# Self attention: key, query and output projections as products of 64 stationary columns in two column halves, bias product over 128 rows

## The reference

```python
attn_in = _adaln(x, cond, ln1_w, ln1_b, g1_w, g1_b, b1_w, b1_b)
q = _heads(xq @ wq)
k, v = jnp.split(ctx @ wkv, 2, axis=-1)
...
q = _rope(q, sq, cq)
k = _rope(k, sk, ck)
sim = jnp.einsum('bhnd,bhmd->bhnm', q, k) * DH ** (-0.5)
a = jax.nn.softmax(sim, axis=-1)
o = jnp.einsum('bhnm,bhmd->bhnd', a, v)
o = o.transpose(0, 2, 1, 3).reshape(xq.shape[0], xq.shape[1], MID)
return o @ wo + bo
```

## Time and profile before

| | us |
|---|---|
| median of 3 runs | 2261.14 (2261.02 to 2263.14) |
| profiled execution, its span | 2262.3 |
| PE busy | 2086.6 (92%) |
| VectorE busy | 1797.4 (79%) |
| ScalarE busy | 1379.8 (61%) |
| self attention | 0 to about 1571 |

### The profile page before, as it was taken

How to read it: one execution, slowest core, us unless ns; L and a number is a source line. 1 busy time by engine, 2 the same in 40 slices (tenths; PEclk the granted TensorE clock), 3 DMA queues, 4 the chain that set the end, 5 groups by cost and what they waited for, 6 DMA issues and landing times. The chain is left out here.

```text
span 2262.3 us, 37701 instructions
## 1 busy us (share of the span) xinstructions
PE 2086.6 (92%) x14808; PEld 891.2 (39%) x14808; DVE 1797.4 (79%) x2799; ACT 1379.8 (61%) x1748; POOL 35.0 (2%) x26
## 2 busy tenths in 40 slices
PE   4799999999999999999999999997379999986999
PEld 2233333334333334433333533334233344444676
DVE  5888999986899997799999699974858888844664
ACT  4577777765777765677677477662647665633442
POOL 1000000000000000000000000000400000000000
PEclk8899999999999999999999999999579999987999
DMA  5010101111110200110110111002423333324111
GB/s 187 29 38 30 45 32 57 39 38 38 57 39 29 67 29 29 48 57 32 46 39 30 48 48 48 29 17 68 121 80 106 116 121 120 124 71 135 38 38 38
DMA packets 102102, 135.83 MB, mean 60 GB/s; under 512 B 36693, under 2 KB 75175, under 8 KB 101927
## 3 DMA queue, kind: packets, MB, share of 16 engines
q1 hardware_dynamic: 101927, 133.43, 18.1%
HBM read 67.89 MB, written 13.11 MB: 36 GB/s over the span
## 5 line engine op out<-in xcount | busy, mean ns | idle before, releaser
L929 ACT ACTIVATE sa_probs<-sa_ps_s 128x1024 f32<-128x1024 f32 x512 | 496.3, 1021 | 217.2 <-PE sa_ps_s L721 217.2
L736 PE MATMUL sa_ps_o<-sa_probs,sa_v_pair 128*64 128x512 f32 x2048 | 534.9, 614 | 7.2 <-DVE sa_mx L1070 7.2
L1083 DVE TENSOR_TENSOR sa_acc<-sa_acc,sa_probs 128x1024 f32<-128x1024 f32 x384 | 452.8, 1220 | 18.2 <-ACT sa_probs L929 8.3
L1070 DVE CUSTOM_DVE_ANT_0 sa_rise<-sa_ps_t,sa_rise 128x512 f32<-128x512 f32 x504 | 327.2, 686 | 141.0 <-PE sa_ps_t L698 138.0
L917 ACT ACTIVATE sa_rise<-sa_ps_t 128x1024 f32<-128x1024 f32 x252 | 257.5, 1022 | 166.3 <-PE sa_ps_t L691 166.1
L714 PE MATMUL sa_ps_s<-sa_hi 64*128 64x512 f16 x1024 | 197.0, 378 | 1.5 <-ACT sa_raw L903 1.5
L714 PE MATMUL sa_ps_s<-sa_hi,sa_lo 64*128 64x512 f16 x1024 | 197.1, 378 | 0.0
L714 PE MATMUL sa_ps_s<-sa_lo,sa_hi 64*128 64x512 f16 x1024 | 197.0, 377 | 0.0
L736 PEld LDWEIGHTS sa_ps_o<-sa_probs,sa_v_pair 128*64 128x64 f32 x2048 | 106.6, 135 | 187.9 <-issue 101.0
L691 PE MATMUL sa_ps_t<-sa_kd,sa_hi 64*128 64x512 f16 x504 | 99.6, 389 | 23.0 <-ACT sa_hi L913 7.7
L691 PEld LDWEIGHTS sa_ps_t<-sa_kd,sa_hi 64*128 64x128 f16 x504 | 26.1, 93 | 206.2 <-issue 162.3
(11 more groups left out here) (327 smaller groups left out, 3935.4 us busy)
## 6 DMA issues: line engine op xcount, KB each, us to landing
sa_swp<-sa_raw SPq DMA_DIRECT2D x124, 256.0 KB, 2.4
sa_inv<-sa_scratch SPq DMA_DIRECT2D x128, 128.0 KB, 2.9
ca_swp<-ca_raw SPq DMA_DIRECT2D x64, 256.0 KB, 2.4
ca_inv<-ca_scratch SPq DMA_DIRECT2D x64, 256.0 KB, 3.9
sa_xs<-in_x SPq DMA_DIRECT2D x4, 1024.0 KB, 6.6
sa_xr<-in_x SPq DMA_DIRECT2D x4, 1024.0 KB, 6.5
cap_xs<-x_after_self SPq DMA_DIRECT2D x4, 1024.0 KB, 7.3
x_after_cross<-ca_xr SPq DMA_DIRECT2D x32, 128.0 KB, 2.1
```

What stands on the lines that cost most here:

```text
L736: ins = pe.matmul(ps_o[rows(x), half(c)], v_pair[:, kt, rows(x)], probs[:, kt % 2, c, half(x)], start=(kt == 0), stop=(kt == NK - 1))
L929: act.activation(probs[:, kt % 2, c, :], ps_s[c][:, :], ACT.Exp, scale=float(DH) ** -0.5).then_inc(s_p, 1)
L1070: dve.tensor_tensor_reduce(out=larger, in0=max_banks(j, t)[:, half(x)], in1=larger, scale=1.0, scalar=-3.0e38, op0=ALU.add, op1=ALU.max, a ...
L1083: dve.tensor_tensor(acc[:, c, :], before, probs[:, kt % 2, c, :], ALU.add).then_inc(s_acc[c], 1)
```

## The change

`project` and `output` call a new function that makes each product as two: the stationary operand is cut into columns 0 to 63 and 64 to 127, which write partitions 0 to 63 and 64 to 127 of the same bank. Both stream the same moving operand. The bias product is cut in the same way, and is over 128 rows instead of 2: `bo_rows` and `two_ones` get 128 rows, zero but for the first two, which are set on VectorE at the start (one memset more, two waits changed). `project_v` is not changed. Cross attention and the feed-forward layer are not changed.

```diff
+def split_product_by_halves(pe, out, k_tiles, lhs, rhs, lhs_at, rhs_at, start=True, stop=True):
+    terms = [(k, a, b) for k in k_tiles for a, b in ((0, 0), (1, 0), (0, 1))]
+    for i, (k, a, b) in enumerate(terms):
+        for h in range(2):
+            part = slice(h * DH, h * DH + DH)
+            ins = pe.matmul(out[part], lhs[a][lhs_at(k)][:, part], rhs[b][rhs_at(k)], start=(start and i == 0),
+                            stop=(stop and i == len(terms) - 1))
+    return ins
...
-        bo_rows = sb("bo_rows", [2, D], F16)
+        bo_rows = sb("bo_rows", [P, D], F16)
...
-        two_ones = sb("two_ones", [2, P], F16)
+        two_ones = sb("two_ones", [P, P], F16)
...
-                split_product(pe, projected(j, i, c), range(KD), (wk, wq)[i], xT, lambda k: (slice(None), k, cols),
-                              lambda k: (slice(None), b, k, half(c))).then_inc(s_kq[i], 1)
+                split_product_by_halves(pe, projected(j, i, c), range(KD), (wk, wq)[i], xT,
+                                        lambda k: (slice(None), k, cols),
+                                        lambda k: (slice(None), b, k, half(c))).then_inc(s_kq[i], 1)
...
-                    pe.matmul(y_bank(b, t), two_ones[:], bo_rows[:], start=True, stop=False)
-                return split_product(pe, y_bank(b, t), ks, (o_hi, o_lo), wo, lambda k: (slice(None), k, ts),
-                                     lambda k: (slice(None), k, slice(None)), False, stop)
+                    for x in range(2):
+                        pe.matmul(y_bank(b, t)[rows(x)], two_ones[:, rows(x)], bo_rows[:], start=True, stop=False)
+                return split_product_by_halves(pe, y_bank(b, t), ks, (o_hi, o_lo), wo, lambda k: (slice(None), k, ts),
+                                               lambda k: (slice(None), k, slice(None)), False, stop)
...
-            pe.wait_ge(s_init, 5)
+            pe.wait_ge(s_init, 7)
...
-            act.activation(bo_rows[:], bo_two[:], ACT.Copy, scale=WS).then_inc(s_bhi, 1)
+            act.wait_ge(s_init, 5)
+            act.activation(bo_rows[0:2], bo_two[:], ACT.Copy, scale=WS).then_inc(s_bhi, 1)
...
-            dve.memset(two_ones[:], 1.0).then_inc(s_init, 1)
+            dve.memset(two_ones[:], 0.0).then_inc(s_init, 1)
+            dve.memset(bo_rows[:], 0.0).then_inc(s_init, 1)
...
-            dve.wait_ge(s_init, 4)
+            dve.wait_ge(s_init, 5)
+            dve.memset(two_ones[0:2], 1.0).then_inc(s_init, 1)
```

More of the change, by code:

```diff
@@ L1194, in _ @@
             dve.wait_ge(s_bhi, 1)
-            dve.scalar_tensor_tensor(out=bo_low[:], in0=bo_two[:], scalar=WS, in1=bo_rows[:], op0=ALU.mult,
+            dve.scalar_tensor_tensor(out=bo_low[:], in0=bo_two[:], scalar=WS, in1=bo_rows[0:2], op0=ALU.mult,
                                      op1=ALU.subtract).then_inc(s_blo, 1)
```

## The result

| | before | after |
|---|---|---|
| median of the runs, us | 2262.09 (2261.02 to 2263.14) | 2245.38 (2244.09 to 2246.13) |
| span of the profiled execution, us | 2262.3 | 2242.2 |

The ratio is 0.9924, with a 95% interval of 0.9910 to 0.9938: 16.7 us faster. The prediction was 17.7 us, 2243.4 us for the median. (The kernel before was timed anew with every comparison; its medians lie between 2261.8 and 2263.1 us.)

A forecast was written before the change was run, and what follows sets the result against it. TensorE was taken to set the pace nearly everywhere, VectorE close behind. Ordinary groups 8.6, output groups 7.5 and tiles behind the loop 1.6 us sum to 17.7 us saved: 2243.4 us median, range 2233 to 2253 us.

The forecast's parts named there:

- step 0: Key projection in each group: only the entry's change of form goes, since `totals` (128*32) follows; 0.11 us.
- step 4: Query projection between two calls of `values`: the whole price of the change of form is saved, 0.26 us.
- The bound from below: A pair of column halves takes the full product's own time: 0.217 us at 512 columns, 0.109 at 256.
- Rival A: Weight loads in column halves are not hidden, 0.05 us more a pair: 44 us slower, 2305 us; chance 0.09.
- Steps 1 and 5: Key and query projections in ordinary groups: 0 us each, since ScalarE's chain from `shift` holds the following `differences`.
- Output groups: Groups 9, 17 and 25, which have output tiles: 2.5 us saved in each, 7.5 us in all three.
- Step 2: In groups with output tiles, entered from `project_v`, which stays 128*128, so one stop stays: about 0.20 us saved.
- Steps 3 and 6: In groups with output tiles, two tiles each with their bias products: 0.41 us saved in each step.
- Ordinary groups, the count: Key and query projections outside groups with output tiles: 24 x 0.11 + 23 x 0.26 = 8.6 us.
- Behind the loop: Output tiles after the groups: 2.40 instead of 2.60 us from bias to bias, 0.20 x 8 = 1.6 us.
- rival C: VectorE takes back step 4's gain beyond its gap, at worst 6.0 us: 2249.5 us; chance 0.12.
- Rival B: Float32 and float16 column halves still stop between them; only bias and tile gain, 5 to 6 us: 2255.5 us; chance 0.08.

The follow-up runs named there:

- the moves of `high`: ScalarE's `high` of steps 1 and 5 put before the step's exponentials: 2225.43 us in the changed kernel, 2250.63 us in the kernel before.
- the last run: Changed kernel with `high` before the exponentials, step 2's value projection in column halves, and VectorE's multiplication by the sines behind the next step's maxima: 2228.60 us.
- the run of half after half: Changed kernel, but each projection and output tile makes all products of the first column half, then all of the second: one run, 2333.35 us.

## Why the prediction was right, point by point

- *The stop.* 0.10 us at each change of form and 0.05 us for the first float32 load: the earlier trace rows gave it, and with the form kept, both are gone. An ordinary group is 0.37 us shorter, as forecast, 0.11 in step 0 and 0.26 in step 4.
- *No cost of halves.* The bound from below was right in all three lengths, 0.216, 0.109 and 0.056 us a pair. Rival A, the loads that are not hidden, would have needed 0.016 us a pair and got none. Its 0.05 us for a load, taken from float32 rows, was also too much: where a load of 64 float16 columns is exposed it costs 0.02 us (last section).
- *Steps 1 and 5.* Nothing came of them, for the reason given; the moves of `high` show both that ScalarE's chain held them and that the saving was there behind it.
- *Output groups.* Forecast 2.5 us each, measured 2.35, 2.35 and 2.47. Two terms were mis-sized. Step 2 gave 0.11 us instead of 0.20. There VectorE's residual stands behind two multiplications; with one of them moved away, and the value projection in halves (the last run), the step is another 0.35 us shorter, while the halves alone left it at 8.45 us. In step 0 of groups 9 and 17 nothing came (6.88 and 6.90 us) where 0.11 was counted. Steps 3 and 6 gave 0.43 each instead of 0.41.
- *Ordinary groups, the count.* 8.2 us instead of 8.6. Without group 0, which was counted at 0.37 and can't be told from the unsteady start, 8.2 had been forecast too, and that is luck: two misses of 0.8 us stand against each other. Groups 8, 16 and 24 were counted at 0. The first two gave 0.24 us each, and group 24, which prepares nothing, is an ordinary group and gave 0.36. In groups 3, 4, 11, 12, 19 and 20, around the preparation of the next sequence's input, step 0 goes from 6.99 to 7.01 us instead of getting shorter by 0.11: 6 x 0.13 = 0.8 us less, which the prediction had not looked at. The timeline of PE shows who holds step 0, here in group 4 before and after:

```profile
265.32 0.39 PE L338 MATMUL sa_ps_t<-xT_hi,sa_wk_hi 128*128 128x512 f16 x1 [0.19 <-DVE sa_mx L1070]
262.70 0.41 PE L350 MATMUL sa_ps_t<-xT_hi,sa_wk_hi 128*64 128x512 f16 x2 [0.19 <-DVE sa_mx L1085]
```

In both kernels the projection waits for VectorE's maxima, so the stop at its entry was never paid there, and the first load, now seen, is 0.01 us longer in halves.
- *Behind the loop.* 1.5 of 1.6 us.
- *VectorE's gap* (rival C) was enough: step 4 was not taken back. The prediction took the gap of 0.25 us for VectorE's only slack between step 3 and step 6, nearly used up by step 4. But 0.21 us of it is left:

```profile
710.85 0.69 DVE L1085 CUSTOM_DVE_ANT_0 sa_rise<-sa_ps_t,sa_rise 128x512 f32<-128x512 f32 x1 [0.21 <-PE sa_ps_t L711]
```

The rest came out of two short waits in step 5, 0.05 us before its maxima and 0.16 us before its additions, which are gone. In step 3 there was no slack: there the next 0.26 us, won in step 2, was lost.
- *Bias over 128 rows and the set-up.* Bias and tile products are 0.109 us apart, so the 128 rows cost nothing, and the bias alone is worth 4.8 us. The set-up is two memsets more and one wait more, as the diff shows, and not one memset; what it costs can't be told in the unsteady start.
- *Rival B's price.* Its sum, 24 x 0.20 + 1.6, is 6.4 us and not 5 to 6. This changes nothing: `values` and the projection follow each other without the 0.10 us that it needed.

## What to carry to other kernels

Read a dense TensorE from start to start, not by its busy time: with a streaming time for each form, every distance that is longer has a name, and a change of form is one of 0.10 us, plus the first load if that is float32. Where products of different forms take turns many times, giving them one form pays even if it doubles the instructions, down to 128 moving columns, provided the halves take turns in the order; a small product of few rows is better padded than left as the odd one. Before counting such a gain, follow what waits behind each place: here half of the places gave nothing until another engine's chain, which a single move of two calls took apart, was out of the way (2225.4 us).

## What the runs showed of the hardware

Two things stand out. Products of different column halves do not start in program order: in the run of half after half, the seventh product started with the third, the 22nd of a tile with the 18th, and one of `values` before two of the projection. And loads of 64 float16 columns in pairs stay hidden behind 0.056 us of streaming, while one that is exposed costs 0.02 us. That is seen where the value projection gives way to the bias in step 2 of group 9 of the changed kernel (timeline of PE):

```profile
496.03 0.22 PE L338 MATMUL sa_ps_t<-sa_wv_lo,xT_hi 128*128 128x128 f16 x1
496.18 0.30 PE L768 MATMUL sa_ps_t<-sa_bo_rows,sa_two_ones 128*64 128x256 f16 x2
496.31 0.28 PE L350 MATMUL sa_ps_t<-sa_wo_hi,sa_o_hi 128*64 128x256 f16 x2
```

From the last whole product to the bias it is 0.15 us, 0.056 of streaming and the rest the stop, and from the bias to the next pair 0.13 us instead of 0.109. Step 0 of group 4 shows the two forms side by side: from the first product of the projection to the second it is 0.23 us in whole products (265.32 to 265.55) and 0.24 us in halves (262.70 to 262.94), against 0.216 between later ones. So the exposed load costs 0.01 us for 128 float16 columns and 0.02 us for 64 in a half.

The Trainium skill has that column tiling turns Fast Weight Load off (page TensorEngine Tiling (Array Packing), Restrictions and Gotchas) and that loads overlap with products "only when row_grp differs" (TensorE: Matmul & The Clock Gate, Part 3). The traces agree with the first: an exposed load of 64 columns takes 0.02 us in halves, one of 128 columns 0.01 us in the whole form, both float16. (The prediction had held float32 against float16 loads, which shows nothing of column tiling.) But as long as it is hidden the slower load costs nothing at 512, 256 or 128 moving columns. The second sentence is contradicted by every projection of the changed kernel, whose halves share all rows and whose loads run one product ahead.
